# Normalisation, learned graph and graph product on one Trainium2 core: copies out of PSUM shared with VectorE, one sum fewer on GpSimd, and another order in quad 0

## The reference

```
h     = relu(layernorm(x, axis=-1))                    # over the 1024 nodes
avg   = h.mean over the 64 batches, per node; x_norm = avg / |avg|
sim   = (x_norm @ x_norm.T + 1) / 2                    # 1024 x 1024
adj   = (sim + gumbel0 > 1 - sim + gumbel1)            # 0 or 1
nmask = clip(adj + adj.T + I, 0, 1)
common = nmask @ nmask.T
struct = common * common / common.max() where (adj or adj.T) and common > 1, else 0
W     = adj * struct;  Wn = dinv * W * dinv            # dinv = deg ** -0.5 of the column sums
out   = x + Wn.T applied to (h @ weight) + bias        # for each of the 64 batches
```

## Time and profile before

| | |
|---|---|
| median of 3 runs | 921.62 us (921.16 to 922.99) |
| the profiled execution, its own time | 921.26 us |
| its span | 919.5 us (1.76 us lie around it) |
| granted TensorE clock | 1.00 of full speed in every slice |
| TensorE, matmuls | busy 887.7 us (97%) |
| VectorE | busy 725.3 us (79%) |
| ScalarE | busy 328.0 us (36%) |
| GpSimd | busy 239.8 us (26%) |

### The profile page before, as it was taken

How to read it: one execution, slowest core, us unless ns; L and a number is a source line. 1 busy time by engine, 2 the same in 40 slices (tenths; PEclk the granted TensorE clock), 3 DMA queues, 4 the chain that set the end, 5 groups by cost and what they waited for, 6 DMA issues and landing times.

```text
span 919.5 us, 12305 instructions
## 1 busy us (share of the span) xinstructions
PE 887.7 (97%) x4563; PEld 761.4 (83%) x4567; DVE 725.3 (79%) x1471; ACT 328.0 (36%) x531; POOL 239.8 (26%) x188
## 2 busy tenths in 40 slices
PE   4999999999999999999999999999999999999997
PEld 3777665788788888888888888888889888988886
DVE  7878858899989797888879787868576758677687
ACT  4999935651221121302121211323333342424130
POOL 4799960500212121111111111302011111111111
PEclk9999999999999999999999999999999999999999
DMA  9999889233436170716344352615233252524122
GB/s 355 382 419 381 328 326 422 81 123 116 137 138 206 69 275 6 269 61 214 105 170 140 135 190 85 225 50 198 77 134 141 90 185 69 183 92 161 46 92 92
DMA packets 37484, 160.25 MB, mean 174 GB/s; under 512 B 3376, under 2 KB 3504, under 8 KB 32176
## 3 DMA queue, kind: packets, MB, share of 16 engines
q1 hardware_dynamic: 37424, 159.46, 46.8%
HBM read 108.07 MB, written 51.38 MB: 173 GB/s over the span
## 4 chain that ended last, share of the span: by engine, by line
PE 79%; DVE 9%; ACT 6%; POOL 3%; issue 2%; DMA 0%; DVEq 0%; ACTq 0%; POOLq 0%
PE ps L1354 69%; PE ps L1303 4%; ACT main L532 4%; DVE bmem L957 3%; POOL main L473 3%; ACT bmem L541 2%; PE ps L1224 2%; DVE stats L750 2%; PE ps L1206 1%; DVE bmem L950 1%; PE ps L1137 1%; PE ps L1284 1%; DVE main L1070 1%; DVE main L1046 1%; DVE bmem L969 0%
## 5 line engine op out<-in xcount | busy, mean ns | idle before, releaser
L1354 PE MATMUL ps<-bmem,main 128*128 128x256 f32 x3136 | 685.1, 379 | 4.0 <-DVE main L1037 2.6
L1354 PEld LDWEIGHTS ps<-bmem,main 128*128 128x128 f32 x3136 | 592.4, 190 | 83.3 <-DVE main L1037 3.5
L500 POOL TENSOR_TENSOR main<-main 128x256 f32<-128x256 f32 x32 | 28.7, 896 | 477.3 <-ACT main L659 424.0
L1037 DVE TENSOR_TENSOR main<-ps,main 128x512 f32<-128x512 f32 x124 | 76.5, 623 | 71.0 <-PE ps L1354 71.0
L490 POOL TENSOR_TENSOR main<-main 128x256 f32<-128x256 f32 (+1 forms) x96 | 91.9, 984 | 139.0 <-DVE main L1030 139.0
L1046 DVE TENSOR_TENSOR main<-main 128x256 f32<-128x256 f32 (+1 forms) x256 | 124.5, 558 | 0.0
L473 POOL TENSOR_TENSOR main<-main 128x1024 f32<-128x1024 f32 x41 | 96.9, 2364 | 23.4 <-ACT main L532 18.5
L619 ACT ACTIVATE ps<-ps 128x512 f32<-128x512 f32 x64 | 33.8, 528 | 159.2 <-PE ps L1354 159.2
L750 DVE BATCH_NORM_STATS2 stats<-main 128x6 f32<-128x512 f32 x128 | 81.2, 674 | 4.5 <-DMA main<-in_x 4.5
L877 DVE TENSOR_TENSOR main<-main 128x256 f32<-128x256 f32 x112 | 48.2, 431 | 44.7 <-PE ps L1354 41.5
L1137 PEld LDWEIGHTS ps<-w_sb,main 128*128 128x128 f32 x560 | 67.0, 194 | 15.0 <-issue 12.0
(11 more groups left out here) (101 smaller groups left out, 541.2 us busy)
## 6 DMA issues: line engine op xcount, KB each, us to landing
main<-in_x SPq DMA_DIRECT2D x92, 512.0 KB, 7.2
main<-in_x SPq DMA_DIRECT2D x32, 1024.0 KB, 6.7
out<-main SPq DMA_DIRECT2D x31, 1024.0 KB, 4.9
main<-spill SPq DMA_DIRECT2D x17, 1024.0 KB, 5.3
spill<-bmem SPq DMA_DIRECT2D x16, 1024.0 KB, 11.9
main<-in_L_gnn_gumbel SPq DMA_DIRECT2D x8, 1024.0 KB, 6.3
spill<-main SPq DMA_DIRECT2D x2, 512.0 KB, 4.6
out<-main SPq DMA_DIRECT2D x1, 512.0 KB, 4.9
```

The costliest lines, as they stand in the source:

```text
L1037: dve.tensor_tensor(at, piece(slot, b), at, ALU.add).then_inc(s, 1)
L1354: last = pe.matmul(piece(slot, b)[:, QUARTER * e:QUARTER * (e + 1)], left_[:, blk(c)], right_[:, c, :], start=slot in FRESH and b < 3 and ...
```

## The change

- `keep` of (5,1), (9,1), (13,1) and (17,1) goes from ScalarE to VectorE (`BY_VECTOR`), ahead of the last `bn_stats` of groups 6, 8, 10 and 12. The copies that ScalarE still makes are done in another order: `keep(p-4, 1)` and then `keep(p-2, 0)` at step p (`LAG = (2, 4)`), where it was `keep(p-3, 1)` and `keep(p-2, 0)`.
- `SPILLED` holds pairs 12 and 25 in place of 8 and 26.
- Pair 23 leaves `BOTH`: GpSimd makes 40 sums, TensorE one more.
- Of the transposes of rows 0 and 1, the 14 that need only the first seven comparisons come ahead of the wait for the eighth.
- In quad 0, slots 0 and 6 get an order of their own, as slot 2 had: the matmuls that need only ready blocks come first.
- VectorE in quad 0: `add_kept(0, 4)` comes ahead of `prepare(6)`, `finish(0, 1)` after one piece of `add_kept(0, 6)` instead of two, and `finish_kept(0, 1)` moves into quad 1, where it stands with `finish_kept(0, 0)` ahead of `finish(1, 0)`.

```diff
-    SPILLED = [0, 1, 2, 3, 5, 7, 8, 9, 11, 13, 15, 17, 19, 21, 23, 26]
+    SPILLED = [0, 1, 2, 3, 5, 7, 9, 11, 12, 13, 15, 17, 19, 21, 23, 25]
+    BY_VECTOR = [5, 9, 13, 17]
+    LAG = (2, 4)
+    def product(p, b):
+        return 2 * SPILLED.index(p) + b
+    MADE = [product(q, b) for p in range(PAIRS) for q, b in ((p - 1, 1), (p, 0)) if q in SPILLED]
+    VECTOR_COPIES = [*(product(p, 1) for p in BY_VECTOR), KEPT - 2, KEPT - 1]
+    SCALAR_COPIES = [product(q, b) for p in range(PAIRS) for q, b in ((p - LAG[1], 1), (p - LAG[0], 0))
+                     if q in SPILLED and product(q, b) not in VECTOR_COPIES]
-    BOTH = [4, 6, 8, 11, 14, 16, 18, 20, 23]
+    BOTH = [4, 6, 8, 11, 14, 16, 18, 20]
...
-                    if p - 3 in SPILLED[:-1]:
-                        keep(p - 3, 1)
-                    if p - 2 in SPILLED[:-1]:
-                        keep(p - 2, 0)
+                    for b in (1, 0):
+                        q = p - LAG[b]
+                        if q in SPILLED and product(q, b) in SCALAR_COPIES:
+                            keep(q, b)
...
                     long_step(t, 6)
+                    for p in BY_VECTOR:
+                        if t == (p + 7) // 2:
+                            keep(p, 1)
                     long_step(t, 7).then_inc(s_bn, 1)
...
             def keep_product(p, b):
-                n = 2 * SPILLED.index(p) + b
-                wait(pe, s_kept, n - 1)
+                n = product(p, b)
+                if n >= 2:
+                    wait_copied(pe, n - 2)
...
-                if quad:
+                if quad == 1:
+                    inner_sums(quad, 3)
+                    finish_kept(0, 0, u_keep, s_g21, 0)
+                    finish_kept(0, 1, v_keep, s_g22, 8)
+                elif quad:
+                    finish_kept(quad - 1, 0, u_keep, s_g21, 16 * quad - 8)
                     inner_sums(quad, 3)
                 finish(quad, 0)
...
                 if quad == 0:
+                    add_kept(quad, 4, v_keep, s_vkeep, s_g22)
                     prepare(6)
                 inner_sums(quad, 6)
...
-            transposes(0)
-            transposes(1)
+            for i in range(2):
+                for j in range(C - 1):
+                    transpose(i, j)
+            pe.wait_ge(s_adj, C)
+            for i in range(2):
+                transpose(i, C - 1).then_inc(s_tr, 1)
...
+                        if slot == 0:
+                            pe.wait_ge(s_comb, 4 * n + 4)
+                            pe.wait_ge(s_scaled, KC)
+                            pe.wait_ge(s_repc, 1)
+                            times(0, 0, 2, 0, q[0, 1], moving[1, 0])
+                            times(0, 0, 2, 1, s4, moving[1, 1])
+                            free(0, 0, 0)
+                            times(0, 0, 0, 0, q[0, 0], moving[0, 0])
+                            pe.wait_ge(s_repc, 2)
...
+                        else:
+                            pe.wait_ge(s_scaled, made_at["T4"])
+                            free(0, 6, 0)
+                            times(0, 6, 0, 0, q[0, 0], moving[0, 0])
+                            free(0, 6, 2)
+                            times(0, 6, 2, 0, q[0, 1], moving[1, 0])
+                            pe.wait_ge(s_comb, 4 * n + 4)
+                            times(0, 6, 2, 1, s4, moving[1, 1])
+                        pe.wait_ge(s_inner, slot + 1)
```

More of the change, by code:

```diff
@@ L299, in odds, with wait_copied, wait_made @@
             return p + 1 - sum(q <= p for q in BOTH)
+        def wait_copied(eng, n):
+            if n in VECTOR_COPIES:
+                eng.wait_ge(s_kept_vector, VECTOR_COPIES.index(n) + 1)
+            else:
+                eng.wait_ge(s_kept, SCALAR_COPIES.index(n) + 1)
+        def wait_made(eng, n):
+            eng.wait_ge(s_hw, MADE.index(n) + 1)
         def wait(eng, s, value):
@@ L528, in relu @@
                 if p - HPAIRS in SPILLED:
-                    act.wait_ge(s_hw, 2 * SPILLED.index(p - HPAIRS) + 2)
+                    wait_made(act, product(p - HPAIRS, 1))
                 for b in range(2):
@@ L678, in _ @@
                 for b in range(4):
[L679 removed]
+                    keep_bank(quad, 2, b, u_keep, 8 if quad == 1 else 16 * quad, s_ukeep)
                     weigh(quad, (2, b))
                 for b in range(4):
[L682 removed]
+                    keep_bank(quad, 3, b, v_keep, 16 if quad == 1 else 16 * quad - 8, s_vkeep)
                     weigh(quad, (3, b))
@@ L750, in long_step, with keep @@
                 return dve.bn_stats(stats[:, t % 2, c // 2, 6 * f:6 * f + 6], xin[:, p % XPAIRS, b, half(f)])
+            def keep(p, b):
+                n = product(p, b)
+                wait_made(dve, n)
+                if HOMES[n] in HOMES[0:n]:
+                    dve.wait_ge(s_spill[HOMES.index(HOMES[n]) // 2], 16)
+                dve.tensor_copy(kept[:, HOMES[n], :], bank(2 + 2 * b, 2)).then_inc(s_kept_vector, 1)
             for t, pairs in enumerate(GROUPS):
@@ L768, in _ @@
                     for b in range(2):
[L769 to L772, removed]
+                        keep(SPILLED[-1], b)
                     whole_chain(t)
@@ L1008, in prepare @@
                     minus(rows_of(T4_ROWS), rows_of(B21_ROWS), rows_of(T2_ROWS), start)
+                    made_at["T4"] = made[0]
                     inner_of(6)
@@ L1113, in _ @@
                     finish_kept(quad, 0, u_keep, s_ukeep, 16 * quad)
-                add_kept(quad, 4, v_keep, s_vkeep, s_g22)
+                if quad:
+                    add_kept(quad, 4, v_keep, s_vkeep, s_g22)
                 if quad + 1 < QUADS:
@@ L1117, in _ @@
                 if quad == 0:
[L1118 to L1122, removed]
+                    add_kept(quad, 6, u_keep, s_ukeep, s_g21, range(1))
+                else:
+                    finish_kept(quad, 1, v_keep, s_g22, 16 * quad + (0 if quad + 1 < QUADS else 8))
+                finish(quad, 1)
                 if quad + 1 < QUADS:
-                    add_kept(quad, 6, u_keep, s_ukeep, s_g21, range(4) if quad else range(2, 4))
+                    add_kept(quad, 6, u_keep, s_ukeep, s_g21, range(4) if quad else range(1, 4))
                     dve.wait_ge(s_g21, 4 * quad + 4)
```

57 lines of the change are left out of this document (28 added, 29 removed).

## The result

| | before | with the change |
|---|---|---|
| median | 922.25 us (4 runs) | 940.89 us (4 runs, 939.62 to 941.6) |
| ratio | | 1.0202, 95% interval 1.0184 to 1.0219 |
| span of the profiled execution | 919.5 us | 939.1 us |
| mean granted TensorE clock | 0.999 | 0.992 |
| TensorE, column sums start | 124.62 us | 145.11 us |

The change makes the kernel 2.0% slower. The direction and the place were forecast, the size was not: 930.8 us was predicted, with 934.5 as the upper end of the range, and it is 18.6 us more than before instead of 9.2. The last two lines of the table say where: stage 1 is 20.5 us longer, everything behind it 0.9 us shorter.

What follows compares the result with a forecast made beforehand. GpSimd was taken to bound stage 1 before the change, ScalarE through TensorE after it. 919.5 + 10.6 - 0.25 - 3.7 + 2.6 = 928.7 us of span, 930.8 us as timed; 8-in-10 range 925 to 934.5.

Steps and rivals of the forecast that it cites:

- What bounds the kernel, and where the change acts: Whole kernel: TensorE nearly full from 280 us on, time open only before; GpSimd decides stage 1's end, TensorE 0.5 behind.
- The stalls of ScalarE: Stage 1, steps 4, 5, 15: ScalarE stalls about 3.6 us for two products; relu of pairs 7 and 17 also wait.
- The rival "faster": Stage 1: GpSimd stays the bound, stalls fit the slack, one sum fewer pays; 917.8 us, chance 0.09.
- The rival by which only the first run of spilled pairs costs: Stage 1: stalls at steps 15 to 17 (6.4) covered, GpSimd ends 3.9 late; 924.2 us, chance 0.10.
- The size of stage 1, +10.6: End of stage 1: column sums start at 135.2 against 124.62, with ScalarE through TensorE deciding.
- +12.5 as the upper end for stage 1: Stage 1's upper bound, if each of some ten new handovers costs 0.2 us; the lower bound was +8.5.
- The rule on the shared port: Stage 1: VectorE copies may block GpSimd, costing it 4.6 us and ending stage 1 13.1 late; taken as nothing.
- Copies on VectorE beside GpSimd: Stage 1: four moved copies cost GpSimd nothing and save ScalarE 3.6 us, with one square root 0.4 late.
- Transposes, -0.25: Stage 2: VectorE's 0.79 us wait for the first transposed row shrinks by 0.25; bounds 0 and -0.6.
- Quad 0, -3.7: Quad 0: TensorE's waits for VectorE shrink by 0.7, 1.9 and 1.1 us, together -3.7.
- Quad 1, +2.6: Quad 1, slot 2: TensorE waits 2.6 us for the memset of piece 3; bounds +1.5 and +4.1.

Runs made afterwards that it cites:

- the experiment with pair 23: Pair 23 put back in BOTH, against the changed kernel with extra matmuls filling TensorE's waits: 934.27 us in a single run.

## Why the prediction was wrong, point by point

- **What bounds the kernel, and where the change acts.** Right. The column sums took the whole loss.
- **The stalls of ScalarE.** Right in mechanism, place and count; LAG alone makes them and LAG alone takes them away (943.52 against 922.35; 918.63 against 940.89). The rival "faster" needed `relu(8)` to start before 43.6; it started at 56.93. The rival by which only the first run of spilled pairs costs falls with the waits of 3.93 and 3.78 at the second.
- **The size of stage 1, +10.6: the step that failed.** The prediction priced each product in a stall at the 1.79 us of the earlier trace rows, where TensorE had not waited. It said itself that these products may start only when a copy is done, so that TensorE waits ahead of them, and did not ask what its clock is after such a wait. In four of the five stalls it is 0.57 to 0.69 over the stretch behind the wait, and two of the three stalls for two products are 5.46 and 5.56 us and not 3.6. The column sums moved by 20.5, 9.9 more than forecast. By the experiment with added matmuls 6.4 of that is the clock. Of the other 3.5, about 2 are handovers that were priced too low: a stall with the clock at 1.00 is 3.93 and not 3.6, one of a single product 2.22 and not 1.8, and pair 18 starts at 91.81 in that experiment where the sum said 89.7. The price was the spacing from start to start, but ScalarE waits for the end of the last matmul, and the rows of the products are 3.84 and 2.05 long. The last 1.3 falls between pairs 18 and 30, where the prediction put the waits at nothing. There `relu(29)` starts 1.0 later than the `relu` ahead of it would let it (126.13 for 122.84 + 2.27), since it waits for product (25,1), and a copy at 103.24 starts 0.2 late; all else in that stretch adds up to 35.6, where 35.5 was forecast. By the experiment with pair 23 about half of that wait is TensorE's full queue, the rest the lag.
- **The bounds.** +12.5 as the upper end for stage 1 let only the handovers grow, and not the duration of the work itself. That is why the range missed. The rule on the shared port was weighed, while the page of the Trainium skill that bore on the size was not: "TensorE: Matmul & The Clock Gate" says in its section "Part 1: The HAM clock gate" that an idle TensorE is set to 1.2 GHz and gets 2.4 GHz back through work. The trace agrees in the main (0.69 and 0.57 of full clock after waits of 3.34 and 4.37 us, 1.00 with the waits filled), though after one wait of 2.75 us the clock stayed at 1.00.
- **Copies on VectorE beside GpSimd.** The term of nothing for GpSimd held: the sums stay at 2.50 (27.46 for 11 with the change; 82.68 for 33, with all four moved copies beside them, with the old lag). What the copies give ScalarE was put too high: the prediction counted their 3.6 but for one square root 0.4 late. In the change the stalls cover the rest (one such wait of 0.32 is left), but with the old lag three square roots wait 0.74 each, and 0.9 arrives at the column sums.
- **Transposes, -0.25.** The wait went from 0.79 to 0.50: 0.29.
- **Quad 0, -3.7.** From the first join to the point at which slot 2's piece 3 of quad 1 is due, TensorE (due at 225.21 + 220 x 0.2161 = 272.8) needs 272.8 - 167.1 = 105.7 us; before it was 256.5 - 147.0 = 109.5. That is 3.8.
- **Quad 1, +2.6.** By starts the wait is 276.02 - 272.8 = 3.2; the memset came 0.5 later than forecast (it ends at 275.97; less the 20.1 by which VectorE's rows here have moved, that is 255.9, not 255.4). The delay is there already at the memset of quad 0, behind sums that take 0.83 to 0.95 beside GpSimd's adds (251.2 to 255.2) in place of 0.42; from there to the memset of quad 1 it is 4.3 more than before, as forecast, 3.5 of it the eight extra adds. The wait lies within its bounds of 1.5 to 4.1. (Of the 2.8 of GpSimd's adds that the prediction sets beside the 4.88 of the earlier trace rows, only 1.8 overlap it, 237.09 to 238.87.) Together stages 2 and 3 gave -0.9, where -1.35 was forecast.

## What to carry to other kernels

When a change makes engines take turns instead of running side by side, price the work of the turn at the clock that TensorE has after its wait, and not at the duration that it has in a full stretch; where it isn't known which clock it will be, the two give the bounds (3.9 and 5.5 us for the stalls here). An order of copies is to be read as a chain through the queue that makes their inputs: a later copy of one buffer is harmless only if nothing asked for right behind it stands in the queue behind that buffer's next use. And when several waits are removed, look for the next deadline on the same engine before adding them up; moving eight adds twice, the second time behind the next deadline, was worth 2.8 us.

## What the hardware showed that I had not expected

- The length of a wait does not by itself tell whether TensorE comes out of it slow. After 2.75 us the two products took 5.47 at one place (38.96 with the change) and 3.84 at another (81.92), and after 2.56 us 5.46 (77.59 with only the lag changed).
- Matmuls whose result nobody reads made the changed kernel 5.7 us faster, by keeping the clock at 1.00 through five waits of 2.75 to 4.37 us.
